# 59 gather tiles of a four-layer graph network, fetched row by row from SyncE and ScalarE

## The reference

```python
x = layernorm(x + L0(x))   # msg = relu(x[src] + edge_attr @ We + be); segment_sum(msg, dst); two dense layers
x = layernorm(x + L1(x))   # four graph attentions a, b, c, d with 8 heads of 16, 32, 16 and 64 channels
x = layernorm(x + L2(x))   # five gated steps: a[dst] += W[etype] h[src]; GRU cell
x = layernorm(x + L3(x))   # segment_sum(weight[rel] h[src] * norm, dst); relu
```

## Time and profile before

| | us |
|---|---|
| median of 3 runs (8169.3 to 8176.95) | 8175.43 |
| the profiled execution | 8184.69 |
| its span, first to last instruction | 8183.3 |
| layer 0, its gathers | 4 to 916 |
| the gathers of a, of b | 1052 to 1985, 2178 to 3188 |
| the gathers of c, of d | 3406 to 4264, 4457 to 5475 |
| POOL busy | 5285.2 (65%) |
| PE, DVE, ACT busy | 5765.4 (70%), 4654.3 (57%), 2316.8 (28%) |
| granted TensorE clock, mean | 0.835 |

### The profile page before, as it was taken

How to read it: one execution, slowest core, us unless ns; L and a number is a source line. 1 busy time by engine, 2 the same in 40 slices (tenths; PEclk the granted TensorE clock), 3 DMA queues, 4 the chain that set the end, 5 groups by cost and what they waited for, 6 DMA issues and landing times.

```text
span 8183.3 us, 141625 instructions
## 1 busy us (share of the span) xinstructions
PE 5765.4 (70%) x50188; PEld 5286.3 (65%) x50188; DVE 4654.3 (57%) x8857; ACT 2316.8 (28%) x6265; POOL 5285.2 (65%) x5490
## 2 busy tenths in 40 slices
PE   5878635887466666478885999988779999823333
PEld 3666535886466665377773889886769999722333
DVE  7777535776487887388884777764122222333333
ACT  0000023443143343044441666651011111112221
POOL 7777777777777776777777777777740000077776
PEclk9989767998588887599995999995889999966666
DMA  5554123332255553133323777762559888711111
GB/s 186 181 171 131 32 69 76 81 79 60 71 145 153 145 147 86 45 86 89 87 76 87 219 218 221 219 168 79 221 228 359 337 335 334 271 29 28 28 28 27
DMA packets 433760, 1151.73 MB, mean 141 GB/s; under 512 B 153430, under 2 KB 227031, under 8 KB 395735
## 3 DMA queue, kind: packets, MB, share of 16 engines
q0 software_dynamic: 225664, 471.04, 23.1%
q1 hardware_dynamic: 205596, 671.39, 22.6%
q10 hardware_dynamic: 1792, 0.23, 0.0%
HBM read 1018.79 MB, written 120.93 MB: 139 GB/s over the span
## 4 chain that ended last, share of the span: by engine, by line
PE 34%; POOL 30%; issue 16%; DVE 11%; DMA 5%; ACT 2%; DVEq 1%; ACTq 0%; SPq 0%; POOLq 0%
POOL pool L1580 16%; PE ps L2282 10%; PE ps L1544 10%; POOL ACC L522 5%; POOL cnt_d L900 5%; PE ps L541 3%; PE ps L1225 2%; DVE ACC L497 2%; POOL pool L522 2%; PE ps L1830 2%; DMA pool<-d_h,srcT_s 2%; ACT ACC L1497 1%; DVE pool L1433 1%; POOL edge_d L1337 1%; DVE pool L1381 1%
## 5 line engine op out<-in xcount | busy, mean ns | idle before, releaser
L1544 PE MATMUL ps<-pool 128*106 128x128 f32 (+2 forms) x19344 | 2402.4, 283 | 50.0 <-DVE pool L1433 50.0
L1544 PEld LDWEIGHTS ps<-pool 128*106 128x106 f32 (+2 forms) x19344 | 2294.6, 170 | 60.3 <-DVE pool L1433 59.8
L1497 ACT ACTIVATE ACC<-ps 72x256 f32 (+1 forms) x2418 | 1012.5, 419 | 1496.2 <-PE ps L1544 1300.8
L522 POOL DMA_INDIRECT ACC<-t,ACC x410 | 387.1, 944 | 1224.4 <-DVE ps L2094 1099.7
L900 POOL DMA_INDIRECT cnt_d<-pool x806 | 843.0, 1046 | 317.2 <-issue 241.2
L1433 DVE TENSOR_TENSOR pool<-pool,ps 128x1024 f32<-128x1024 f32 (+1 forms) x807 | 927.4, 1208 | 0.0
L1580 POOL DMA_INDIRECT pool<-b_h,srcT_s x806 | 765.0, 949 | 245.6 <-issue 232.2
L1580 POOL DMA_INDIRECT pool<-d_h,srcT_s x806 | 764.3, 948 | 245.6 <-issue 177.0
L497 DVE TENSOR_TENSOR ACC<-ACC,ps 65x128 f32 (+1 forms) x1612 | 454.2, 282 | 799.5 <-PE ps L541 573.5
L1580 POOL DMA_INDIRECT pool<-a_h,srcT_s x738 | 708.6, 960 | 224.7 <-issue 215.3
L2282 PE MATMUL ps<-pool,ACC 128*128 128x192 bf16 x8600 | 768.6, 250 | 68.7 <-DMA ACC<-cnt_d 68.7
(11 more groups left out here) (346 smaller groups left out, 8849.6 us busy)
## 6 DMA issues: line engine op xcount, KB each, us to landing
ACC<-cnt_d SPq DMA_DIRECT2D x172, 1600.0 KB, 8.7
pool<-cnt_d SPq DMA_DIRECT2D x88, 1600.0 KB
cnt_d<-pool SPq DMA_DIRECT2D x26, 3200.0 KB, 12.1
ACC<-t SPq DMA_DIRECT2D x1536, 0.2 KB
ACC<-key_d SPq DMA_DIRECT2D x17, 1280.0 KB
ACC<-key_d SPq DMA_DIRECT2D x21, 768.0 KB
ACC<-t ACTq DMA_DIRECT2D x896, 0.2 KB
ACC<-key_d SPq DMA_DIRECT2D x26, 512.0 KB
```

Of the source, the lines that this page charges most:

```text
L522: g.indirect_dma_start(out=gb[b][:, k, :], out_offset=None, in_=table, in_offset=bass.IndirectOffsetOnAxis(ap=idx[:, c:c + 1], axis=0)).th ...
L1497: a.activation(win[:, 0:NPL, bass.ds(reg, 128)], pl[0].rearrange("p (i c) -> p i c", c=128), ACT.Copy).then_inc(*(tile_out if last else A) ...
L1544: mm = t.matmul(o, gbr[:, tile % RT, M * i:M * i + M], oh, start=True, stop=True)
```

## The change

59 tiles leave POOL's list: the first tile of groups 4, 8, ... 48 in `a`, `b` and `d` (12 each), of groups 6, 12, ... 48 in `c` (8), and of 15 groups of layer 0. Their 128 rows are fetched by single-row DMAs into a strip `rows_held` or `held_l0` outside the ring, some of them in each pair or group, well ahead. When the ring's slot is free, one DMA copies the strip into it (`sync_held_tile`, `sync_tile_l0`, `scalar_tile_l0`). In `d` the strip has 116 rows, and the last 12 go straight into the ring's slot. Row numbers come from two new inputs, eight at a time into registers (16 at a time on ACT).

```diff
+PAIRS_OF = {"a": 2, "b": 2, "c": 3, "d": 2}
+STAGED_OF = {q: list(range(2 * PAIRS_OF[q], 50, 2 * PAIRS_OF[q])) for q in "abcd"}
+ROWS_FROM, SP_ROWS, ACT_ROWS = 7, 24, 16
...
+        def sync_rows_l0(gi):
+
+            for e0 in range(SP_ROWS * (gi - ROWS_FROM), SP_ROWS * (gi - ROWS_FROM + 1), 8):
+                i, p0 = e0 // 128, e0 % 128
+                if e0 >= 0 and i < len(SP_L0):
...
+                    _, regs = nc.values_load_multi_w_load_instructions(
+                        sp_nos[i % 2][0:1, p0:p0 + 8], engines=[mybir.EngineType.SP], min_val=0, max_val=NP - 1,
...
+                    for e in range(8):
+                        s.dma_start(held_l0[i % 2][p0 + e:p0 + e + 1, :],
+                                    I["x"][bass.ds(regs[e], 1), :]).then_inc(*sp_staged[i % 2].one())
...
+        def sync_tile_l0(u):
+
+            i = SP_L0.index(u)
+            s.wait_ge(sp_staged[i % 2].sem, 16 * 128 * (i // 2 + 1))
+            s.wait_ge(eam.sem, 2 * (u - GB0) + 1)
+            s.dma_start(gb0[u % GB0][:, 0, :], held_l0[i % 2]).then_inc(*sp_put.one())
...
@@ scalar_l0, after the relu of group gi
+                if gi + 5 in ACT_L0:
+                    scalar_tile_l0(gi + 5)
+                scalar_rows_l0(gi)
@@ tensor_l0, before the gathered rows are added
+                if gi in SP_L0:
+                    t.wait_ge(sp_put.sem, 16 * (SP_L0.index(gi) + 1))
+                if gi in ACT_L0:
+                    t.wait_ge(act_put.sem, 16 * (ACT_L0.index(gi) + 1))
@@ sync_l0, at the end of a group
+                if gi + 4 in SP_L0:
+                    sync_tile_l0(gi + 4)
+                sync_rows_l0(gi)
@@ gat
+            def sync_rows(i, p0, p1, place, landed):
+
+                for e0 in range(p0, p1, 8):
+                    m = min(8, p1 - e0)
...
+                    for e in range(m):
+                        s.dma_start(place[e0 + e:e0 + e + 1, :], ht[bass.ds(regs[e], 1), :]).then_inc(*landed.one())
+
+            def sync_held_rows(p):
+
+                i, part = p // PAIRS, p % PAIRS
...
+                each = -(-128 // PAIRS // 8) * 8
...
+                sync_rows(i, each * part, min(each * part + each, HELD), rows_held[i % 2], rows_in_held[i % 2])
+
+            def sync_held_tile(gi):
+
+                i, c = STAGED.index(gi), GR[gi][0]
+                s.wait_ge(rows_in_held[i % 2].sem, 16 * HELD * (i // 2 + 1))
+                if c >= RT:
+                    s.wait_ge(tile_mm.sem, tm0 + set_of(c - RT))
+                s.dma_start(gbr[0:HELD, c % RT, 0:RW], rows_held[i % 2][0:HELD, :]).then_inc(*tile_put.one())
+                sync_rows(i, HELD, 128, gbr[:, c % RT, 0:RW], tile_put)
+                sync_row_numbers(i + 2)
...
@@ vector_edge_scores
+                if gi in STAGED:
+                    v.wait_ge(tile_put.sem, PUT * (STAGED.index(gi) + 1))
@@ gpsimd_pass
-                        if c >= RT and c % S == 0:
+                        if c == c0 and gi in STAGED:
+                            continue
+                        if c >= RT and (c % S == 0 or (c == c0 + 1 and gi in STAGED)):
                             g.wait_ge(tile_mm.sem, tm0 + set_of(c - RT))
@@ sync_pass, at the end of a pair
+                    if gi in STAGED:
+                        sync_held_tile(gi)
+                    sync_held_rows(gi // 2)
```

More of the change, by code:

```diff
@@ L41 @@
 ACT_GROUPS = [u + 1 if u in ROW_GROUPS else u for u in range(10, NG, 8)]
+PAIRS_OF = {"a": 2, "b": 2, "c": 3, "d": 2}
+STAGED_OF = {q: list(range(2 * PAIRS_OF[q], 50, 2 * PAIRS_OF[q])) for q in "abcd"}
+ROWS_FROM, SP_ROWS, ACT_ROWS = 7, 24, 16
+SP_L0 = [u for u in (ROWS_FROM - (-128 * (i + 1) // SP_ROWS) + 4 for i in range(NG)) if u < NG]
+ACT_L0 = [u for u in (ROWS_FROM + 128 * (i + 1) // ACT_ROWS + 5 for i in range(NG)) if u < NG]
+L0_STAGED = SP_L0 + ACT_L0
 NSP, NROW = len(ROW_GROUPS), len(ROW_GROUPS) + len(ACT_GROUPS)
@@ L111, in build @@
         cst = sb("cst_s", [128, 1676])
+        row_nos = [ns[0:1, 520 + 128 * j:648 + 128 * j].bitcast(I32) for j in range(2)]
+        nos_in = [dsig("row_numbers0_in"), dsig("row_numbers1_in")]
         hx = {16: [cst[32 * r:32 * r + 8, 0:144] for r in range(3)], 32: [cst[32 * r:32 * r + 8, 144:444] for r in range(3)],
@@ L507, in gpsimd_tile_flags, with gpsimd_gather @@
                     in_=tile_flag[:, j, :], in_offset=None).then_inc(*flagged.one())
-        def gpsimd_gather(table, idx, gb, arrived, read, parts, free=0, ready=None, tiles=lambda gi: K):
+        def gpsimd_gather(table, idx, gb, arrived, read, parts, free=0, ready=None, tiles=lambda gi: K, first=lambda gi: 0):
             nb = len(gb)
@@ L516, in gpsimd_gather @@
                     gpsimd_tile_flags()
-                for k in range(tiles(gi)):
+                for k in range(first(gi), tiles(gi)):
                     c = gi * K + k
-                    part = [i for i, (k0, m) in enumerate(parts) if k0 == k]
+                    part = [i for i, (k0, m) in enumerate(parts) if max(k0, first(gi)) == k]
                     if part and gi >= nb:
@@ L660, in gathered_tiles, with first_gathered @@
             return K - PG if gi >= FIRST else K
+        def first_gathered(gi):
+            return 1 if gi in L0_STAGED else 0
         def arrivals_l0(gi):
-            return 16 * sum(gathered_tiles(x) for x in range(gi % GB0, gi + 1, GB0))
+            return 16 * sum(gathered_tiles(x) - first_gathered(x) for x in range(gi % GB0, gi + 1, GB0))
+        held_l0 = [wl[:, 1388:1452], wl[:, 1452:1516], wl[:, 1516:1580], wl[:, 0:64]]
+        sp_nos, act_nos = ([ns[0:1, 256 * q + 128 * j:256 * q + 128 * j + 128].bitcast(I32) for j in range(2)] for q in range(2))
@@ new lines, in build, with sync_numbers_l0, scalar_numbers_l0 @@
+        sp_nos_in, act_nos_in = nos_in, [dsig(f"l0_act_numbers{j}_in") for j in range(2)]
+        sp_staged, act_staged = ([dsig(f"l0_{q}_staged{j}") for j in range(2)] for q in ("sp", "act"))
+        sp_put, act_put = dsig("l0_sp_tile_put"), dsig("l0_act_tile_put")
+        def sync_numbers_l0(i):
+            if i < len(SP_L0):
+                s.dma_start(sp_nos[i % 2], I["srcR0"][i:i + 1, :]).then_inc(*sp_nos_in[i % 2].one())
+        def scalar_numbers_l0(i):
+            if i < len(ACT_L0):
+                a.dma_start(act_nos[i % 2], I["srcR0"][len(SP_L0) + i:len(SP_L0) + i + 1, :]).then_inc(*act_nos_in[i % 2].one())
@@ new lines, in sync_rows_l0 @@
+        def sync_rows_l0(gi):
+            for e0 in range(SP_ROWS * (gi - ROWS_FROM), SP_ROWS * (gi - ROWS_FROM + 1), 8):
+                i, p0 = e0 // 128, e0 % 128
+                if e0 >= 0 and i < len(SP_L0):
+                    if p0 == 0 and i >= 2:
+                        s.wait_ge(sp_put.sem, 16 * (i - 1))
+                    if p0 == 0:
+                        s.wait_ge(sp_nos_in[i % 2].sem, 16 * (i // 2 + 1))
+                    _, regs = nc.values_load_multi_w_load_instructions(
+                        sp_nos[i % 2][0:1, p0:p0 + 8], engines=[mybir.EngineType.SP], min_val=0, max_val=NP - 1,
+                        skip_runtime_bounds_check_because="sources are node numbers")
+                    for e in range(8):
+                        s.dma_start(held_l0[i % 2][p0 + e:p0 + e + 1, :],
+                                    I["x"][bass.ds(regs[e], 1), :]).then_inc(*sp_staged[i % 2].one())
+                    if p0 == 120:
+                        sync_numbers_l0(i + 2)
@@ new lines, in sync_tile_l0, with scalar_rows_l0 @@
+        def sync_tile_l0(u):
[3 more added lines that the diff above has]
+            s.dma_start(gb0[u % GB0][:, 0, :], held_l0[i % 2]).then_inc(*sp_put.one())
+        def scalar_rows_l0(gi):
+            e0 = ACT_ROWS * (gi - ROWS_FROM)
+            i, p0 = e0 // 128, e0 % 128
+            if e0 >= 0 and i < len(ACT_L0):
+                if p0 == 0 and i >= 2:
+                    a.wait_ge(act_put.sem, 16 * (i - 1))
+                if p0 == 0:
+                    a.wait_ge(act_nos_in[i % 2].sem, 16 * (i // 2 + 1))
+                _, regs = nc.values_load_multi_w_load_instructions(
+                    act_nos[i % 2][0:1, p0:p0 + ACT_ROWS], engines=[mybir.EngineType.Activation], min_val=0, max_val=NP - 1,
+                    skip_runtime_bounds_check_because="sources are node numbers")
+                for e in range(ACT_ROWS):
+                    a.dma_start(held_l0[2 + i % 2][p0 + e:p0 + e + 1, :],
+                                I["x"][bass.ds(regs[e], 1), :]).then_inc(*act_staged[i % 2].one())
+                if p0 + ACT_ROWS == 128:
+                    scalar_numbers_l0(i + 2)
@@ L665, in by_products, with scalar_tile_l0 @@
+        def scalar_tile_l0(u):
+            i = ACT_L0.index(u)
+            a.wait_ge(act_staged[i % 2].sem, 16 * 128 * (i // 2 + 1))
+            a.wait_ge(eam.sem, 2 * (u - GB0) + 1)
+            a.dma_start(gb0[u % GB0][:, 0, :], held_l0[2 + i % 2]).then_inc(*act_put.one())
         def by_products(u):
@@ L760, in scalar_l0 @@
             a.wait_ge(*mark["l0_ready"])
```

(47 more changed lines are left out.)

## The result

The changed kernel takes **8262.9 us** (median of 4 runs, 8260.3 to 8267.3), the kernel before 8172.4 beside it on the same chip (8165.8 to 8177.0): a ratio of 1.0113, 95% interval 1.0097 to 1.0129. It is 1.1% slower; the forecast was 8138, faster. The profiled execution has a span of 8261.8 us against 8183.3.

A forecast was written before the change was run, and what follows sets the result against it. POOL's gathers bound `a`, `b`, `d` at 1.25 us a tile; in layer 0 SP would become last. +7 - 15 - 15 - 0 - 15 = -38 us gives 8138 us on the median; 8 in 10: 8105 to 8205.

The forecast's parts named there:

- layer 0's sum: Layer 0, 48 groups: SP needs 14.5 us a group against 13.8 now, so layer 0 ends 7 us later.
- old work and copies: Layer 0, SP's round: edge features, keys, zero fills, flag load and store, gaps 1.9 us a group; copies add 0.1.
- rows above 0.45: Sign of a wrong forecast: a row costing SP over 0.45 us, where 0.42 was taken from layer 3.
- the 26 (19 + 7): Layer 0: 19 us of POOL gathers removed, and 7 us regained in six faster groups after the rows end.
- the keys: Layer 0: behind the waiting SP stand edge features and keys, and PE and VectorE wait for these.
- The 9 us that I had at 0: Stretch from layer 0's last relu to the first logit of `a`: forecast difference 0.
- SP becomes the bound: Loads of 8 cost 1.232 us; layer 0 +73, `a` +38, `b` keeps 13, `d` 8: 8265; chance 0.20 (above 8192).
- its last clause (rows beside the fills): Rows costing more than 0.42 beside the 3.2 MB fills would also make SP the bound; no separate size or chance.
- The attentions: Gathers removed at 1.25 us a tile: `a`, `b` and `d` 15 us faster each, `c` 0.
- SP's pair within its margin in `a`: In `a`, late pairs last 34.4 us, SP falls back 11 us in all; the lists have about 20 us left.
- The rival that rows crowd one DMA engine there: In `d`, one engine at 97%, gathers late, 15 us lost plus some 20: 8175; chance 0.20 shared with other cases.
- The load of 8, taken at 0.78: SP's register load of 8 row numbers: 0.78 us, between lines giving 0.72 and 0.81.

The follow-up runs named there:

- fills behind layer 0: The change, with all but the first three of the 26 zero fills issued behind layer 0's loop: 8274.1 us (one run), last relu 901.9.
- layer 0 only: The change with only layer 0's 15 tiles fetched row by row, attentions gathering as before: 8297.6 us, ratio 1.0142 to the kernel before.

## Why the prediction was wrong

**The step that failed is layer 0's sum, "24 x 0.42 = 10.1 us".** Over the 48 rounds SP spent 577.7 us on 1151 rows (from one instruction's start to the next one's), 141.4 on 144 loads and 100.5 on the rest. A round by terms:

| term | forecast | the change | fills behind layer 0 |
|---|---|---|---|
| 24 rows | 10.08 | 12.05 | 10.2 |
| 3 loads | 2.43 | 2.95 | 2.5 |
| old work and copies | 2.0 | 2.09 | 1.1 |
| sum | 14.5 | 17.1 | 13.8 |

Three quarters of the 2.6 us are rows. The 0.42 came from layer 3, where no fill runs; it is right for a row that stands clear of one. The evidence against it was in my own rows: the flag store of 3.39 us behind a fill. I booked it as the price of that store. It was the price of a place: what SP issues in the 12 us behind a fill is held up, and in the kernel before only the store and now and then an edge feature stood there. The new rows filled that place with some five issues of about 1 us for every fill (105 over 22 fills), and a row came to 0.50 us in the mean: the prediction had named rows above 0.45 as a sign of being wrong.

**What followed from it** went as the prediction said, but for the keys. 48 x (17.1 - 13.8) = 157 us late at group 55; the last relu 117 late, so 40 were covered or regained, against the 26 (19 + 7) that I had. Behind the late SP stood the edge features (PE: 159.5 us). For the keys, of which the prediction said the same, VectorE has no wait there. The 9 us that I had at 0 are POOL's: its first counts, which before began 5 us ahead of the last relu, now wait for VectorE's last counts and begin 3 us behind it. VectorE comes to these late because it stands at PE (from 145 to 1045 us, the first line; 71.8 us in the kernel before):

```profile
DVE pool L774 <- PE ps L803: 208.3, 51, 12.1
...
POOL cnt_d L989 <- DVE pool L369: 70.0, 1, 70.0
```

**The rival "SP becomes the bound"** gave 8265, and 8263 was measured, but not by its sum. It priced the load at 1.23 us and so had +73 in layer 0 and +38 in `a`; the load took 0.79 and `a` gained 16.5. Its mechanism and its last clause (rows beside the fills) were right; the agreement of the totals is chance. Had I priced that clause, with 1 us for some five rows of every second group, 5 x 0.75 / 2 = 1.9 us a group, the round would have been 16.4 and layer 0 48 x 2.6 - 26 = 99 us later. The five and the 1 us come from the changed kernel: the store's row told that a place behind a fill is dear, not how many issues stand in it.

**The attentions were right** in mechanism and size: 1.25 us a tile, SP's pair within its margin in `a`, and in `c` nothing that can be told from its clock. `d` gave 9 to 12 us of 15. The rival that rows crowd one DMA engine there falls: `d` gained, and the gathers' mean stayed at 0.948. A single row is moved by one engine (two packets each); what that costs in `d` is at most the 3 to 6 us that it fell short. The Trainium skill (DMA: Bandwidth & Descriptors, "Why a DMA increments its semaphore by 16 and not by 1") says that a copy issued by SP or ACT runs on the lowest-numbered k of the core's 16 engines; no run here shows on which one the rows ran. The load of 8, taken at 0.78 between the ends 0.27 and 1.23, took 0.786.

On the fills, the rows say that SP's and ACT's issues slow together while a fill is moved (DMA share 0.96), and SP's also when ACT issued the fill. Whether an issue is held up by the busy engines or by something else that a fill keeps busy, no run tells apart. The Trainium skill (DMA: Bandwidth & Descriptors, "Issuing engines are not separate DMA queues") says that DMAs run on the same 16 engines whoever starts them, and that another issuer saves only the time of the sequencer, usually small beside the DMA. The trace agrees with the first half. In the second, "usually" matters: for rows of 256 bytes the sequencer's 0.42 us is what SP's round is made of. Moving the fills to ACT was worth 0.7% of the kernel, of which layer 0 gave 35 us (1038.4 to 1003.1) and `c`, unexplained, 21.

A version faster than both came out: 16 rows a group by SP, 12 tiles of layer 0 in all, 0.69% below the kernel before (0.52 to 0.86). That all 15 tiles would give more with fills out of the way is not shown: layer 0 ended at 901.9 against 907.3, and the fills then stand behind it.

## What to carry to other kernels

An engine that has much idle time is not free for work in small pieces: set its round, dear places included, against the pace of the loop, and ask for each new issue what stands ahead of it there. When a short DMA issue shows a long duration, do not book it to that instruction; look at what was issued just before, and price everything that will stand in that place. Below the threshold such an addition costs nothing, and above it each 0.1 us counts in every turn of the loop: here 16 rows gained 0.7%, and 24 lost 1.1%.

## What the runs showed of the hardware

- While a fill of 3.2 MB was moved (12 us, DMA share 0.96), a row's DMA issue on SP took up to 2.5 us instead of 0.23 (in the change; up to 3.7 with 16 rows a group), and on ACT up to 1.5 instead of 0.21; the number of such issues on SP (105 of 1152 rows, 109 of 768) went with the fills, not with the rows; with longer loads, which take a share of that time, it was 51 and 82. Register loads stretch too: a load of 8 from 0.79 to 2.4 us, a load of 24 from 1.8 to 6.1.
- A store issued 1.1 us behind a fill in the same queue took 3.4 to 3.6 us to issue and 13.4 us to land; with the fill issued by ACT it stood over 15 us behind one, and took 0.5 and 5.2 (medians). The one store 7 us behind a fill of ACT's took 1.5 and 8.5.
- While PE waited for the edge features, between two fills, its granted clock fell to 0.67 (fifth row of the stretches, between the levels of 1.2 and 2.4 GHz); over layer 0 it was 0.86 in the change, 0.91 before and 0.95 with the fills moved away. PE's busy time grew by 8 us only, so the lower clock does not account for the wait.
- Attention `c` took 850.4, 840.7 and 827.6 us (before, layer 0 only, fills issued by ACT) with PE busy for 679, 667 and 654 us over the same matmuls, at a granted clock of 0.93, 0.95 and 0.97, means between the two levels.
